# A selective state-space stack on one core: who adds up the scaled states, and in which order the projections run

## The chip, the cores and the metric

The program runs on one NeuronCore of a Trainium2 chip. Its five engines have queues of their own and meet at semaphores: TensorE (PE) for matrix products, VectorE (DVE), ScalarE (ACT), GpSimd (POOL) and SyncE (SP), which issues most DMAs. The metric is the device time of one execution in microseconds (us); a kernel is run several times and the median is compared.

## The reference

The input is one sequence x of 8192 positions with 512 channels, in fp32. Two parts follow, each as x + layernorm(part(layernorm(x))).

The first part is a stack of two Mamba layers, and it takes nearly all the time. With 1024 inner channels and 16 states each, a layer computes:

```python
xz = einsum('bld,ed->ble', x, W_in);  xc, z = split(xz, 2)
u = silu(causal depthwise conv of 4 taps (xc) + b_c)
dt, Bm, Cm = split(einsum('bld,ed->ble', u, W_x), [32, 48])
delta = softplus(einsum('blr,dr->bld', dt, W_dt) + b_dt)
dA = exp(delta * A);  dBu = delta * Bm * u
h = dA_t * h + dBu_t;  y_t = sum over n of h[:, n] * C_t[n]    # for every position t
y = (y + u * D) * silu(z);  out = einsum('bld,od->blo', y, W_out)
```

The second part is a soft mixture of 16 experts with 16 slots each. The change doesn't touch it.

## The kernel before, in words

A layer is cut into 16 chunks of T = 512 positions, so there are 32 chunks; the index G counts them. A chunk has 32 groups k: two halves of four 128-channel blocks, times 16 states. Each group needs four scans of 512 positions, one a block; VectorE does two blocks in one instruction (`scan`, L1289). So a chunk has 128 slots s = 4k + b, one for each scan of a block, and 64 double scans, p = s // 2. All orders are tables over these slots:

- ScalarE makes the decays exp(delta A) into a PSUM ring of four (`decay_of`, L928), and the first column of the scan's input (`head`, L938). It may be two double scans ahead.
- GpSimd makes the inputs delta u B (`inputs`, L1172) in a ring of three double scans.
- TensorE turns the states of a group, one 128-position tile j at a time, so that positions stand on the partitions (`turn_states`, L666). It writes the turned tile, 128 x 512, to one of two PSUM banks in turn (`BANK`, `turn_bank`); the bank is free when the engine that reads tile i - 2 is done.
- The turned tile is multiplied by C, one number per partition. VectorE does six of eight tiles and adds in the same instruction into `acc` (`add_state`, L1319; the first of a sum is a scaling, L1317). ScalarE does the others (`by_act`, `product`, L958) into one of three pairs of buffers `prod`. These are j = 0 of even k and j = 3 of odd k, `V_AT = (0, 3)`. A pair q is the two tiles of k = 2q and 2q + 1.
- GpSimd adds the pairs of a half to the first of them (`add_pair`, L1214: seven in a half), and at the half's end `join` (L1223) adds the total to `acc`. `V_SUM_AT` and `JOIN_AT` say behind which input each stands.
- TensorE turns the sum back (`turn_y`: a product with a diagonal of D, then four turned pieces added in PSUM), and VectorE multiplies it by silu(z) (`gate_y`, L1328). `Y_AT` has the slots of these y tiles.

Between these run the projections of this chunk and the next, in the order of `ORDER`. `timetable` gives each matmul a slot of TensorE by weights, and each result a slot in ScalarE's program, `TAKE_LAG` = 3 later plus what `TAKE_LATER` says. Two PSUM banks serve them in turn (`RING` = 2): a projection may start when ScalarE has taken the one two places ahead in `ORDER`. The silus need another table than the exponentials, so one is a table load, an activation over four blocks and a table load back (`silu_u`, `silu_z`); `SILU_LATER` moves the four of a chunk. By the table before, silu of z stands in ScalarE's slots 114 and 2 of the next chunk, silu of u in 42 and 66. `W_AT` has GpSimd's steps on delta (`sum_delta` L1154, `product` L1161), at p13, p16, p20, p23 and p46, p49, p52, p56.

The chunks G = 0 to 13 also carry the layernorm of chunk G + 2: its steps on ScalarE (`NORM_AT`) and four turned tiles on TensorE (`norm`, L694). Chunk 31 has no next chunk to project for.

## Time and profile before

| | us |
|---|---|
| median of 3 runs (7706.72 to 7708.32) | 7707.89 |
| the profiled execution | 7704.26 |
| its span | 7702.5 |
| VectorE busy in the span | 7066.7 (92%) |
| TensorE busy | 7011.1 (91%) |
| GpSimd busy | 6663.3 (87%) |
| ScalarE busy | 6029.3 (78%) |

The mean granted clock of TensorE is 0.982 of full speed. A row of the timeline gives the start (us from the span's start), the duration, engine, line of the kernel, operation, output and inputs, the number of instructions merged in it, and in brackets the idle time of the engine ahead of it with the instruction that the trace names as its end. A row that merges n instructions runs from the start of the first to the end of the last. Neighbouring instructions of an engine overlap a little, since the next is started before the last has written its end. The first scan starts at 100.4 us and the last at 7120.4 us.

### The profile page before, as it was taken

What the parts mean: (1) busy time and instruction counts of PE and PEld (TensorE: products, weight loads), DVE (VectorE), ACT (ScalarE), POOL (GpSimd) and SP (SyncE); (2) the same over time, 40 slices, a digit from 0 to 9 for tenths busy, and PEclk for the clock granted to TensorE, in tenths of its full rate; (3) what the DMA queues carried; (4) which work ended last, traced back from release to release, by engine and by line L of the source; (5) the groups of instructions that cost most, each with busy time, mean ns of one, the idle gap of its engine ahead of it and who ended that gap; (6) DMA issues with size and microseconds to landing.
All of it is one profiled execution on the core that took longest, in us unless ns stands there. A gap on an engine that the chain in (4) does not pass through costs nothing. (4 is left out here: it accounts for less than half of the span.)

```text
span 7702.5 us, 98947 instructions
## 1 busy us (share of the span) xinstructions
PE 7011.1 (91%) x29580; PEld 3860.8 (50%) x29580; DVE 7066.7 (92%) x6228; ACT 6029.3 (78%) x13267; POOL 6663.3 (87%) x3115
## 2 busy tenths in 40 slices
PE   7899999999999999999999999999999999987799
PEld 3444544544554454544554555444554544444664
DVE  5999999999999999999999999999999999999755
ACT  7788888888788888877888888777888887776564
POOL 5999999999999999999999999999999999998010
PEclk9999999999999999999999999999999999998999
DMA  3222222222222222222222222222222222221765
GB/s 107 77 85 84 79 85 72 79 85 81 86 78 86 78 73 83 83 87 70 87 88 69 76 69 77 73 75 70 75 77 68 76 71 73 76 72 52 257 229 183
DMA packets 282695, 684.05 MB, mean 89 GB/s; under 512 B 37872, under 2 KB 38128, under 8 KB 254384
## 3 DMA queue, kind: packets, MB, share of 16 engines
q1 hardware_dynamic: 252464, 626.31, 24.7%
q10 hardware_dynamic: 29696, 51.40, 1.8%
q8 instruction: 239, 3.92, 0.2%
q14 instruction: 296, 2.42, 0.1%
HBM read 508.76 MB, written 168.82 MB: 88 GB/s over the span
## 5 line engine op out<-in xcount | busy, mean ns | idle before, releaser
L1172 POOL TENSOR_TENSOR bu<-w,b_rep 128x1022 f32<-128x1022 f32 x2048 | 4797.9, 2361 | 416.6 <-DVE h L1289 413.1
L1289 DVE TENSOR_TENSOR_SCAN h<-decay,bu 128x1024 f32<-128x1024 f32 x2048 | 4644.0, 2277 | 216.0 <-ACT decay L928 71.0
L666 PEld LDWEIGHTS turn<-ident_m,h 128*128 128x128 f32 x16384 | 1963.2, 143 | 2697.1 <-issue 1287.4
L928 ACT ACTIVATE decay<-delta,neg_a 128x511 f32<-128x511 f32 x4096 | 2664.9, 684 | 738.8 <-DVE h L1289 735.6
L666 PE MATMUL turn<-ident_m,h 128*128 128x128 f32 x16384 | 2550.5, 280 | 489.5 <-DVE acc L1319 352.2
L1319 DVE SCALAR_TENSOR_TENSOR acc<-turn,c_now,acc 128x512 f32<-128x512 f32 x2816 | 1966.5, 733 | 139.8 <-PE turn L666 138.8
L1214 POOL TENSOR_TENSOR prod<-prod 128x1024 f32<-128x1024 f32 x448 | 1060.5, 2367 | 10.1 <-ACT prod L958 10.1
L588 PE MATMUL proj<-conv_in,conv_diag 128*128 128x512 f32 x1984 | 995.4, 601 | 67.6 <-ACT halo L818 67.6
L588 PE MATMUL proj<-x_conv,w_in 128*128 128x512 f32 x2048 | 1034.4, 602 | 9.3 <-ACT u L825 8.1
L588 PE MATMUL proj<-x_gate,w_in 128*128 128x512 f32 x2048 | 1012.4, 594 | 0.0
L958 ACT ACTIVATE prod<-turn,c_now 128x512 f32<-128x512 f32 x1024 | 696.3, 683 | 317.4 <-PE turn L666 296.5
L588 PE MATMUL proj<-zy,w_out 128*128 128x512 f32 x1024 | 518.5, 601 | 0.0
L588 PE MATMUL proj<-w_out,zy 128*128 128x512 f32 x1024 | 512.1, 599 | 0.9 <-DVE zy L1328 0.9
L938 ACT COPY bu<-h_first 128x2 f32<-128x2 f32 x2048 | 384.6, 188 | 63.8 <-ACT stage L877 26.2
L588 PEld LDWEIGHTS proj<-conv_in,conv_diag 128*128 128x128 f32 x1984 | 317.1, 191 | 213.5 <-ACT halo L818 107.8
L588 PEld LDWEIGHTS proj<-x_conv,w_in 128*128 128x128 f32 x2048 | 331.1, 193 | 141.8 <-issue 107.7
L588 PEld LDWEIGHTS proj<-x_gate,w_in 128*128 128x128 f32 x2048 | 327.3, 191 | 107.6 <-issue 107.6
L1154 POOL TENSOR_TENSOR delta<-delta,w 128x1024 f32<-128x1024 f32 x128 | 302.5, 2363 | 41.5 <-ACT w L862 41.5
L808 ACT ACTIVATE conv_diag<-ident_m,par 128x128 f32<-128x128 f32 x992 | 315.1, 390 | 0.4
L1161 POOL TENSOR_TENSOR w<-delta,u 128x1024 f32<-128x1024 f32 x128 | 303.4, 2370 | 0.3
L674 PE MATMUL turn<-u_back,d_diag 128*128 128x512 f32 x512 | 283.3, 635 | 2.5 <-DMA u_back<-u_rows 1.2
L588 PE MATMUL proj<-u,w_x 128*64 128x512 f32 x512 | 270.9, 623 | 10.2 <-ACT u L829 10.2
(167 smaller groups left out, 5721.6 us busy)
## 6 DMA issues: line engine op xcount, KB each, us to landing
b_rep<-b_rows SPq DMA_DIRECT2D x1024, 256.0 KB, 3.2
u_rows<-u SPq DMA_DIRECT2D x64, 1024.0 KB, 4.3
u_back<-u_rows SPq DMA_DIRECT2D x256, 256.0 KB, 3.5
x_gate<-xt SPq DMA_DIRECT2D x32, 1024.0 KB, 7.7
xt<-stage ACTq DMA_DIRECT2D x128, 256.0 KB, 2.4
x_conv<-xt SPq DMA_DIRECT2D x31, 1024.0 KB, 6.3
x_gate<-in_x_dram SPq DMA_DIRECT2D x16, 1024.0 KB, 5.1
x_l<-in_x_dram SPq DMA_DIRECT2D x16, 1024.0 KB, 10.0
```

The source lines that it names most:

```text
L588: mm = pe.matmul(out[0:lhs.shape[1], :], lhs, rhs, start=n == 0, stop=n == count - 1)
L666: mm = pe.transpose(out[:, b * P:(b + 1) * P], h[:, (G * GROUPS + k) % H_RING, b, j * P:(j + 1) * P], ident[:])
L808: act.activation(conv_diag[:, b % 2, k, :], ident[:], ACT.Copy, scale=par[:, STATES + k, b:b + 1])
L928: act.activation(decay[:, (G * SLOTS_BODY + s) % DEC_RING, 1:T], delta[:, blk, 1:T], ACT.Exp, scale=neg_a[:, n, blk:blk + 1]).then_inc(dec ...
L938: act.copy(bu[:, (G * PAIRS + p) % BU_RING, :, 0], h_first[:, hf, n, 2 * pr:2 * pr + 2]).then_inc(head_set, 1)
L958: act.activation(prod[:, V_BUFFER[q], k % 2, :], turn[:, BANK[tile], :], ACT.Copy, scale=c_now[:, j, n:n + 1]).then_inc(v_done, 1)
L1154: pool.tensor_tensor(delta[:, lo:lo + 2, :], delta[:, lo:lo + 2, :], w[:, lo:lo + 2, :], ALU.add).then_inc(delta_set, 1)
L1161: pool.tensor_tensor(w[:, lo:lo + 2, :], delta[:, lo:lo + 2, :], u[:, lo:lo + 2, :], ALU.mult).then_inc(w_set, 2)
L1172: pool.tensor_tensor(bu[:, (G * PAIRS + s // 2) % BU_RING, :, 1:T], w[:, blk:blk + 2, 1:T], b_rep[:, g % B_RING, 1:T].unsqueeze(1).to_broa ...
L1214: pool.tensor_tensor(total, total, prod[:, V_BUFFER[q]], ALU.add).then_inc(vsum_set, 1)
L1289: dve.tensor_tensor_scan(h[:, (G * GROUPS + k) % H_RING, 2 * pr:2 * pr + 2, :].rearrange("p b t -> p (b t)"), decay[:, at:at + 2, :].rearr ...
L1319: dve.scalar_tensor_tensor(out, src, scalar, out, ALU.mult, ALU.add).then_inc(x_done, 1)
```

## The change

- ScalarE's two tiles of a pair are now j = 3 of even k and j = 0 of odd k: `V_AT = (3, 0)`. Only for the first two groups of a half it is different: of k = 0 ScalarE takes both j = 3 and j = 0, and writes them into `acc` itself, and of k = 1 VectorE takes all four.
- Pair 1 of a half is written to that half's own total, and GpSimd adds pairs 2 to 7 to it, out of one spare buffer. There are no joins.
- `turn_y` adds six turned pieces: four of `acc`, two of the total. It waits for both.
- VectorE's first addition for j = 0 and j = 3 waits for ScalarE's tile in `acc`, and ScalarE's first write of a half waits for the last y tile of that half before.
- `ORDER` has the norm turns in other places, y weighs more, and takes, silus, y tiles, diagonals and two lists of loads and stores are moved. By the new tables silu of z stands in ScalarE's slots 110 and 126, silu of u in 46 and 62, and the y tiles of the second half in slots 16, 24, 32, 40.

```diff
@@ -41,19 +41,19 @@
-         ('conv_half', 7, 0), ('conv', 6, 0), ('conv', 7, 0), ('norm', 0, 0), ('out', 0, 0), ('norm', 1, 8),
-         ('out', 1, 0), ('x_proj', 0, 0), ('norm', 2, 0), ('norm', 3, 0), ('turn_c', 0, 0), ('delta_next', 0, 0),
-         ('delta_next', 1, 0), ('out', 2, 0), ('delta_next', 2, 0), ('delta_next', 3, 4), ('out', 3, 0), ('gate', 0,
+         ('conv_half', 7, 0), ('conv', 6, 0), ('conv', 7, 0), ('norm', 0, 0), ('out', 0, 0), ('out', 1, 0),
+         ('x_proj', 0, 0), ('norm', 1, 0), ('turn_c', 0, 0), ('delta_next', 0, 0), ('norm', 2, 0),
+         ('delta_next', 1, 0), ('norm', 3, 0), ('out', 2, 0), ('delta_next', 2, 0), ('delta_next', 3, 4), ('out', 3, 0), ('gate', 0,
 SLOTS_BODY = GROUPS * HB
 PAIRS = SLOTS_BODY // 2
 TAKE_LAG, TAPS_LEAD, XDBL_LAG, CONV_LAG, PROD_LAG = 3, 2, 3, 3, 2
-TAKE_LATER = {('out', 0): -1, ('gate', 0): 1, ('gate', 2): 2, ('turn_c', 0): -1, ('conv', 5): -1, ('delta', 5): -1}
-SILU_LATER = (6, 6, 4, 4)
-V_SUM_AT = (10, 10, 10, 10, 10, 10, 10, 9, 9, 9, 10, 10, 10, 10, 10, 9)
-JOIN_AT = (41, 72)
+TAKE_LATER = {('conv_half', 1): -1, ('conv_half', 2): -1, ('out', 0): 0, ('norm', 0): -1, ('gate', 0): 1, ('gate', 2): 2, ('turn_c', 0): -1, ('conv', 5): -1,
+              ('delta', 5): -1}
+SILU_LATER = (8, 2, 1, 0)
+V_SUM_AT = 9
 W_AT = {13: ('sum', 2), 16: ('product', 2), 20: ('sum', 3), 23: ('product', 3), 46: ('sum_next', 0), 49:
         ('product_next', 0), 52: ('sum_next', 1), 56: ('product_next', 1)}
@@ -76,12 +76,12 @@
-Y_AT = ((116, 118, 122, 124), (20, 28, 36, 44))
-DIAG_AT = {106: (0, 0), 110: (0, 1), 119: (0, 2), 121: (0, 3), 12: (1, 0), 17: (1, 1), 26: (1, 2), 34: (1, 3)}
-U_LOAD_AT = {25: [(0, 0)], 26: [(0, 1)], 30: [(0, 2)], 31: [(0, 3)], 3: [(1, 0)], 4: [(1, 1)], 7: [(1, 2)], 9: [(1, 3)]}
-U_STORE_AT = {12: 0, 18: 1}
+Y_AT = ((116, 118, 121, 124), (16, 24, 32, 40))
+DIAG_AT = {104: (0, 0), 108: (0, 1), 119: (0, 2), 122: (0, 3), 9: (1, 0), 13: (1, 1), 22: (1, 2), 30: (1, 3)}
+U_LOAD_AT = {25: [(0, 0)], 26: [(0, 1)], 30: [(0, 2)], 31: [(0, 3)], 2: [(1, 0)], 3: [(1, 1)], 6: [(1, 2)], 8: [(1, 3)]}
+U_STORE_AT = {13: 0, 18: 1}
@@ -110,7 +110,7 @@
-WEIGHT = {"x_proj": 1.1, "delta": 1.25, "delta_next": 1.25, "turn_c": 0.5, "norm": 0.5, "state": 0.55, "y": 1.6}
+WEIGHT = {"x_proj": 1.1, "delta": 1.25, "delta_next": 1.25, "turn_c": 0.5, "norm": 0.5, "state": 0.55, "y": 1.9}
@@ -164,20 +164,26 @@
 PROJ_PROLOGUE = NB + 1 + 1 + HB + NORM_AHEAD * KD
-V_AT = (0, 3)
+V_AT = (3, 0)
 HALF_Q = STATES // 2
-V_BUFFER = (0, 1, 2, 1, 2, 1, 2, 1, 2, 1, 0, 1, 0, 1, 0, 1)
+
+
+SPARE = 2
+V_BUFFER = tuple(q // HALF_Q if q % HALF_Q == 1 else SPARE for q in range(GROUPS // 2))
 def by_act(tile):
-    return tile[0] == "state" and tile[2] == V_AT[tile[1] % 2]
+    what, k, j = tile
+    if what == "state" and k % STATES < 2:
+        return k % STATES == 0 and j in V_AT
+    return what == "state" and j == V_AT[k % 2]
 def emptied_before(q):
-    old = max(o for o in range(-len(V_BUFFER), q) if V_BUFFER[o] == V_BUFFER[q])
-    pair = old % len(V_BUFFER)
-    return ("join", pair // HALF_Q) if pair % HALF_Q == 0 else ("pair", pair), old < 0
+
+    old = q - 1 if (q - 1) % HALF_Q > 1 else q - 3
+    return "pair", old % (GROUPS // 2)
 V_TAKE = [[] for _ in range(SLOTS_BODY)]
@@ -212,13 +218,11 @@
     at, carried = [[] for _ in range(PAIRS)], []
     for q in range(GROUPS // 2):
-        mine = [(4 * q + V_SUM_AT[q], ("pair", q))] if q % HALF_Q else []
-        if q % HALF_Q == HALF_Q - 1:
-            mine.append((JOIN_AT[q // HALF_Q], ("join", q // HALF_Q)))
-        for p, op in mine:
-            at[p % PAIRS].append(op)
+        if q % HALF_Q > 1:
+            p = 4 * q + V_SUM_AT
+            at[p % PAIRS].append(("pair", q))
             if p >= PAIRS:
-                carried.append(op)
+                carried.append(("pair", q))
     return at, carried
@@ in turn_y @@
-        def turn_y(out, joined, X, hf, b):
+        def turn_y(out, added, summed, X, hf, b):
             n = y_number(X, hf, b)
             pe.wait_ge(dd_set, n + 1)
             pe.wait_ge(uback_in[n % 2], (n // 2 + 1) * 16)
             pe.matmul(out, d_diag[:, n % 2, :], u_back[:, n % 2, :], start=True, stop=False)
-            pe.wait_ge(vsum_set, joined)
+            pe.wait_ge(x_done, summed)
             for j in range(J):
-                mm = pe.matmul(out[:, j * P:(j + 1) * P], acc[:, hf, j, b * P:(b + 1) * P], ident[:], start=False, stop=j == J - 1,
+                pe.matmul(out[:, j * P:(j + 1) * P], acc[:, hf, j, b * P:(b + 1) * P], ident[:], start=False, stop=False,
+                          is_transpose=True)
+            pe.wait_ge(vsum_set, added)
+            for odd in range(2):
+                j = V_AT[odd]
+                mm = pe.matmul(out[:, j * P:(j + 1) * P], prod[:, hf, odd, b * P:(b + 1) * P], ident[:], start=False, stop=odd == 1,
                                is_transpose=True)
             mm.then_inc(turn_full, 1)
@@ in turn_tile @@
-                turn_y(out, sum_base(G, kind) + (kind.sums.index(("join", x)) + 1 + C_PROD), G - x, x, j)
+                added = sum_base(G, kind) + (kind.sums.index(("pair", LAST_Q[x])) + 1 + C_PROD)
+                summed = dve_base(G, kind) + (kind.turns.by_dve["state", x * STATES + STATES - 1, J - 1] + 1 + C_TURN)
+                turn_y(out, added, summed, G - x, x, j)
@@ in product @@
-            emptied, in_last = emptied_before(q)
-            if k % 2 == 0 and not (kind.first and in_last):
-                behind = in_last and emptied not in SUMS_CARRIED
-                at = SUMS.index(emptied) - len(SUMS) if behind else kind.sums.index(emptied)
-                act.wait_ge(vsum_set, sum_base(G, kind) + (at + 1 + C_PROD))
-            act.activation(prod[:, V_BUFFER[q], k % 2, :], turn[:, BANK[tile], :], ACT.Copy,
-                           scale=c_now[:, j, n:n + 1]).then_inc(v_done, 1)
+            hf, begins = q // HALF_Q, q % HALF_Q == 0
+            if begins and j == V_AT[1] and not kind.first:
+                old = "y", hf, HB - 1
+                behind = TURN_TILES if hf == 0 else 0
+                act.wait_ge(turn_full, turn_base(G, kind) + (ALL_TURNS.index[old] + 1 - behind))
+            if k % 2 == 0 and q % HALF_Q > 1 and not (kind.first and q == 2):
+                act.wait_ge(vsum_set, sum_base(G, kind) + (kind.sums.index(emptied_before(q)) + 1 + C_PROD))
+            out = acc[:, hf, j, :] if begins else prod[:, V_BUFFER[q], k % 2, :]
+            act.activation(out, turn[:, BANK[tile], :], ACT.Copy, scale=c_now[:, j, n:n + 1]).then_inc(v_done, 1)
...
@@ in add_pair, join @@
-            total = prod[:, V_BUFFER[q - q % HALF_Q]]
-            pool.tensor_tensor(total, total, prod[:, V_BUFFER[q]], ALU.add).then_inc(vsum_set, 1)
-        def join(G, kind, op):
-            hf, done = op[1], sum_base(G, kind) + kind.sums.index(op) + C_PROD
-            pool.wait_ge(vsum_set, done)
-            last = "state", hf * STATES + STATES - 1, 2
-            pool.wait_ge(x_done, dve_base(G, kind) + (kind.turns.by_dve[last] + 1 + C_TURN))
-            both = acc[:, hf, V_AT[0]:V_AT[1] + 1:V_AT[1] - V_AT[0], :]
-            pool.tensor_tensor(both, both, prod[:, V_BUFFER[hf * HALF_Q]], ALU.add).then_inc(vsum_set, 1)
+            total = prod[:, q // HALF_Q]
+            pool.tensor_tensor(total, total, prod[:, SPARE], ALU.add).then_inc(vsum_set, 1)
@@ in add_state @@
@@ -1300,8 +1299,11 @@
             scalar, src, out = c_now[:, j, n:n + 1], turn[:, BANK[tile], :], acc[:, hf, j, :]
             if k == 0 or k == HALF_C:
                 dve.wait_ge(c_set, 2 * G + (k // HALF_C + 1))
+            begun = "state", hf * STATES, j
             first, before = False, ("state", k - 1 - by_act(("state", k - 1, j)), j)
-            if before[1] < hf * STATES:
+            if before[1] < hf * STATES and by_act(begun):
+                dve.wait_ge(v_done, act_base(G, kind) + (kind.turns.by_act[begun] + 1 + C_PROD))
+            elif before[1] < hf * STATES:
                 first = True
                 old = "y", hf, HB - 1
```

What moves, at three places. First GpSimd, in the second half of a second-layer chunk, from the input of p42 before (p38 after) to the first exponent of the next chunk; `delta<-delta,w` and `w<-delta,u` are the delta steps, `prod<-prod` a pair's sum. Before:

```order
L1172 TENSOR_TENSOR bu<-w,b_rep 128x2x511 x4
L1214 TENSOR_TENSOR prod<-prod 128x1024
L1154 TENSOR_TENSOR delta<-delta,w 128x1024
L1172 TENSOR_TENSOR bu<-w,b_rep 128x2x511 x3
L1161 TENSOR_TENSOR w<-delta,u 128x1024
L1172 TENSOR_TENSOR bu<-w,b_rep 128x2x511 x2
L1214 TENSOR_TENSOR prod<-prod 128x1024
L1172 TENSOR_TENSOR bu<-w,b_rep 128x2x511
L1154 TENSOR_TENSOR delta<-delta,w 128x1024
L1172 TENSOR_TENSOR bu<-w,b_rep 128x2x511 x2
L1181 TENSOR_TENSOR a_first<-neg_a,delta 128x64
```

and after:

```order
L1185 TENSOR_TENSOR bu<-w,b_rep 128x2x511 x8
L1167 TENSOR_TENSOR delta<-delta,w 128x1024
L1185 TENSOR_TENSOR bu<-w,b_rep 128x2x511 x3
L1174 TENSOR_TENSOR w<-delta,u 128x1024
L1185 TENSOR_TENSOR bu<-w,b_rep 128x2x511
L1227 TENSOR_TENSOR prod<-prod 128x1024
L1185 TENSOR_TENSOR bu<-w,b_rep 128x2x511 x2
L1167 TENSOR_TENSOR delta<-delta,w 128x1024
L1185 TENSOR_TENSOR bu<-w,b_rep 128x2x511 x2
L1227 TENSOR_TENSOR prod<-prod 128x1024
L1194 TENSOR_TENSOR a_first<-neg_a,delta 128x64
```

The sum of pair 9 ahead of the first delta step is gone (as is the join four inputs ahead of it), and the sums of pairs 10 and 11 stand one input earlier.

Then ScalarE in the same chunk, around the silu of u's second half, `u<-u`; `stage<-proj` is the take of output projection 0, `u<-proj,par` that of conv 7. Before:

```order
L958 ACTIVATE prod<-turn,c_now 128x512 x2
L938 COPY bu<-h_first 128x2
L928 ACTIVATE decay<-delta,neg_a 128x511 x2
L969 COPY h_last<-h 128x4
L877 COPY stage<-proj 128x512
L879 DMA xt<-stage 128x512
L938 COPY bu<-h_first 128x2
L928 ACTIVATE decay<-delta,neg_a 128x511 x2
L829 ACT_TABLE_LOAD
L829 ACTIVATE u<-u 128x2048
L772 ACT_TABLE_LOAD
L938 COPY bu<-h_first 128x2
```

and after:

```order
L837 ACTIVATE u<-proj,par 128x512
L950 COPY bu<-h_first 128x2
L940 ACTIVATE decay<-delta,neg_a 128x511 x2
L841 ACT_TABLE_LOAD
L841 ACTIVATE u<-u 128x2048
L784 ACT_TABLE_LOAD
L950 COPY bu<-h_first 128x2
L940 ACTIVATE decay<-delta,neg_a 128x511 x2
L982 COPY h_last<-h 128x4
L950 COPY bu<-h_first 128x2
```

The silu stood behind the take of output projection 0, and now stands behind conv 7, ahead of that take.

Last ScalarE at the start of a second-layer chunk: the silu of z's second half, `zy<-zy`, conv taps, `conv_diag`, and the first pair of scaled tiles. Before:

```order
L928 ACTIVATE decay<-delta,neg_a 128x511 x2
L871 ACT_TABLE_LOAD
L871 ACTIVATE zy<-zy 128x2048
L772 ACT_TABLE_LOAD
L808 ACTIVATE conv_diag<-ident_m,par 128x128 x4
L938 COPY bu<-h_first 128x2
L928 ACTIVATE decay<-delta,neg_a 128x511 x2
...
L958 ACTIVATE prod<-turn,c_now 128x512
L808 ACTIVATE conv_diag<-ident_m,par 128x128 x4
L958 ACTIVATE prod<-turn,c_now 128x512
```

and after:

```order
L940 ACTIVATE decay<-delta,neg_a 128x511 x2
L879 COPY zy<-proj 128x512
L883 ACT_TABLE_LOAD
L883 ACTIVATE zy<-zy 128x2048
L784 ACT_TABLE_LOAD
L950 COPY bu<-h_first 128x2
L940 ACTIVATE decay<-delta,neg_a 128x511 x2
...
L972 ACTIVATE prod<-turn,c_now 128x512 x2
L820 ACTIVATE conv_diag<-ident_m,par 128x128 x4
```

The silu has moved ahead by two double scans and stands behind gate 7. The two scaled tiles of a pair, which had taps between them, stand together.

## Rows read from the trace of the kernel before

**Rows 1.** Windows: busy time of each engine, one chunk each, last chunk third.

```profile
2326.32:2548.54 222.22, 203.45 (x870) 110.05 (x869) 209.42 (x169) 184.04 (x411) 206.95 (x98) 1.00 0.25 81
4519.92:4737.11 217.19, 201.51 (x853) 108.15 (x852) 208.99 (x169) 174.28 (x384) 206.56 (x97) 1.00 0.23 73
6910.62:7122.60 211.98, 163.00 (x694) 101.66 (x692) 207.40 (x167) 137.80 (x292) 192.97 (x87) 0.81 0.19 60
```

**Rows 2.** Timeline of GpSimd: the same join in two neighbouring chunks, twice.

```profile
2348.20 2.35 POOL L1223 TENSOR_TENSOR acc<-acc,prod 128x1024 f32<-128x1024 f32 x1
...
2570.42 2.36 POOL L1223 TENSOR_TENSOR acc<-acc,prod 128x1024 f32<-128x1024 f32 x1
...
4541.80 2.34 POOL L1223 TENSOR_TENSOR acc<-acc,prod 128x1024 f32<-128x1024 f32 x1
...
4758.99 2.35 POOL L1223 TENSOR_TENSOR acc<-acc,prod 128x1024 f32<-128x1024 f32 x1
```

**Rows 3.** VectorE's groups by line: shapes, count, busy us, mean ns, idle before.

```profile
L1289 DVE TENSOR_TENSOR_SCAN h<-decay,bu 128x1024 f32<-128x1024 f32 x2048 | 4644.0, 2277 | 216.0 <-ACT decay L928 71.0 <-PE turn L666 68.5 <-POOL bu L1172 64.1
L1319 DVE SCALAR_TENSOR_TENSOR acc<-turn,c_now,acc 128x512 f32<-128x512 f32 x2816 | 1966.5, 733 | 139.8 <-PE turn L666 138.8
L1317 DVE TENSOR_SCALAR acc<-turn,c_now 128x512 f32<-128x512 f32 x256 | 183.1, 736 | 19.7 <-PE turn L666 17.8
...
L1346 DVE TENSOR_SCALAR u<-conv_in,par 128x512 f32<-128x512 f32 x8 | 4.4, 547 | 28.9 <-ACT conv_in L816 28.9
```

**Rows 4.** GpSimd's groups by line: the sums of pairs.

```profile
L1214 POOL TENSOR_TENSOR prod<-prod 128x1024 f32<-128x1024 f32 x448 | 1060.5, 2367 | 10.1 <-ACT prod L958 10.1
```

**Rows 5.** Timeline of VectorE, second-layer chunk: scans p51, p52, p55 and p56.

```profile
4690.13 2.29 DVE L1289 TENSOR_TENSOR_SCAN h<-decay,bu 128x1024 f32<-128x1024 f32 x1 [0.45 <-POOL bu L1172]
...
4694.75 2.29 DVE L1289 TENSOR_TENSOR_SCAN h<-decay,bu 128x1024 f32<-128x1024 f32 x1 [1.03 <-PE turn L666]
...
4704.30 2.29 DVE L1289 TENSOR_TENSOR_SCAN h<-decay,bu 128x1024 f32<-128x1024 f32 x1 [0.27 <-POOL bu L1172]
...
4708.92 2.29 DVE L1289 TENSOR_TENSOR_SCAN h<-decay,bu 128x1024 f32<-128x1024 f32 x1 [1.02 <-ACT decay L928]
```

**Rows 6.** Timeline of GpSimd at the same place: inputs p51, p52 and p53, delta sum.

```profile
4687.58 2.35 POOL L1172 TENSOR_TENSOR bu<-w,b_rep 128x1022 f32<-128x1022 f32 x1
4689.89 2.35 POOL L1154 TENSOR_TENSOR delta<-delta,w 128x1024 f32<-128x1024 f32 x1
4692.20 4.66 POOL L1172 TENSOR_TENSOR bu<-w,b_rep 128x1022 f32<-128x1022 f32 x2
```

**Rows 7.** Timeline of ScalarE around silu of u, and VectorE's scans p34, p35.

```profile
4628.30 0.58 ACT L877 COPY stage<-proj 128x512 f32<-128x512 f32 x1 [2.23 <-PE proj L588]
...
4630.69 1.28 ACT L829 ACT_TABLE_LOAD   x1
4631.98 1.92 ACT L829 ACTIVATE u<-u 128x2048 f32<-128x2048 f32 x1
...
4635.31 1.29 ACT L928 ACTIVATE decay<-delta,neg_a 128x511 f32<-128x511 f32 x2
...
4636.69 4.47 DVE L1289 TENSOR_TENSOR_SCAN h<-decay,bu 128x1024 f32<-128x1024 f32 x2 [2.28 <-PE turn L666]
```

**Rows 8.** Timeline of VectorE in the chunk's start, and of ScalarE there.

```profile
4546.40 0.75 DVE L1319 SCALAR_TENSOR_TENSOR acc<-turn,c_now,acc 128x512 f32<-128x512 f32 x1 [0.75 <-PE turn L666]
...
4560.88 0.75 DVE L1319 SCALAR_TENSOR_TENSOR acc<-turn,c_now,acc 128x512 f32<-128x512 f32 x1 [0.98 <-PE turn L666]
...
4554.95 1.27 ACT L808 ACTIVATE conv_diag<-ident_m,par 128x128 f32<-128x128 f32 x4
4556.37 0.69 ACT L958 ACTIVATE prod<-turn,c_now 128x512 f32<-128x512 f32 x1
```

**Rows 9.** Timeline of TensorE and VectorE, first-layer chunk, around p38 and p39.

```profile
2464.01 0.66 PE L694 MATMUL proj<-ident_m,x_gate 128*128 128x128 f32 x4 [2.10 <-ACT spare_m L843]
...
2465.14 1.41 DVE L1319 SCALAR_TENSOR_TENSOR acc<-turn,c_now,acc 128x512 f32<-128x512 f32 x2 [2.08 <-PE turn L666]
```

18 lines of the change are left out of this document (7 added, 11 removed).

## The prediction

> **What bounds the kernel now.** I read the windows first, one for a chunk of each layer and one for the last chunk. In a first-layer chunk VectorE is busy 209.42 of 222.22 us, in a second-layer chunk 208.99 of 217.19 us; GpSimd follows with 206.95 and 206.56 us [rows 1]. The same GpSimd sum comes back after 222.22 us in the first layer (2348.20 to 2570.42) and after 217.19 us in the second (4541.80 to 4758.99), so these are the periods of a chunk [rows 2]. VectorE is the bound, and what can be won is its idle time: 12.80 us a chunk in the first layer, 8.20 us in the second. The state-space stage has 32 chunks. The 14 first of them carry the next chunks' normalization and have the long period; 17 have the short one; the last has no projections for a next chunk and takes 211.98 us [rows 1]. All idle time together is 14 x 12.80 + 17 x 8.20 = 319 us.
>
> Then I read VectorE's timeline for where it waits in a second-layer chunk, and the other engines at the same moments. I count a chunk's 64 double scans from p0 to p63.
> - Before p51, p52, p55 and p56 it waits 0.45, 1.03, 0.27 and 1.02 us, together 2.77 [rows 5]. The trace names GpSimd for two of them, TensorE and ScalarE for the others. But GpSimd has no gap there: the input of p51 is ready at 4689.93 and the scan starts at 4690.13; a delta sum of 2.35 us stands in front of the next input, which ends at 4694.5, and p52 starts at 4694.75 [rows 5, 6]. All four are GpSimd's.
> - Before p34 it waits 2.28 us [rows 7]. ScalarE waited 2.23 us for TensorE's output projection, then ran the silu of u with its two table loads (1.28 + 1.92 + 1.28 = 4.48 us) and came to the decays of p34 late. The trace names TensorE; but the decays end at 4636.60 (4635.31 + 1.29), and the scan starts at 4636.69.
> - The rest, 8.20 - 2.77 - 2.28 = 3.15 us, lies mostly in the first 24 scans, where an accumulation waits for a turned tile. The two longest are 0.75 and 0.98 us [rows 8]. There ScalarE is late: between the two scaled tiles of a pair it makes conv taps (1.27 us), and the tile it has not taken holds one of the two PSUM banks of the turns.
> - In the first layer there is 2.08 us more before the accumulations of p39: TensorE stands 2.10 us until ScalarE has emptied the x_proj bank, since two norm turns follow x_proj in one slot [rows 9]. 12.80 - 2.77 - 2.28 - 2.08 = 5.67 us are left for the rest there.
>
> **The change part by part.**
>
> GpSimd loses four of its 16 sums a chunk: the two joins and pairs 1 and 9. One takes 2.35 us [rows 2, 4], so GpSimd goes from 206.6 to about 197.3 us of work. The joins themselves are worth little: that of the second half sits at p8, that of the first at p41, ahead of places where GpSimd catches up again. What counts is pair 9 at p45, right ahead of the stretch in which four delta steps, at 2.35 us each, make GpSimd late. Worked from p43, where it is level with the scans: without pair 9 it has 2.35 us more, and the four waits of 2.77 us shrink to 0.4. But the silu of z's first half now stands at slot 110 instead of 114, behind three gates and a product that waits for GpSimd's sum. I expect ScalarE to be about 0.8 us late at p56. Gain 2.77 - 0.4 - 0.8 = 1.6 us. Ends: 0, if ScalarE takes over the whole wait, and 2.77.
>
> The silu of u's second half moves from slot 66 to 62, ahead of the take of out 0. ScalarE no longer waits 2.23 us ahead of it, and the scan behind it has two accumulations in front. The silu costs ScalarE 4.48 us and the next decays 1.3. When ScalarE is level, the decays of a scan are ready 3.4 us ahead of it, and the next scan starts 3.5 us later (a scan of 2.2 and two accumulations of 0.65): 6.9 against 5.8 us, so it just fits. I take 2.1 of the 2.28 us, with ends 0.5 and 2.3.
>
> The chunk's start: the silu of z's second half moves from slot 2 of the next chunk to slot 126, where ScalarE has lead, and two conv_half takes come a slot earlier. Each pair of scaled tiles now stands in neighbouring slots with nothing long between them (before, taps, a conv_half or an exponential stood there in most pairs). Adding up ScalarE's work from slot 126 on, with its durations from the timeline, I find it ahead of every scan of p0 to p12 by 1 us or more in the second layer, and level with it around p8 in the first, where the normalization's sums are added. Gain 2.4 of 3.15 us in the second layer, 4.2 of 5.67 in the first. Ends: 0 and all of it.
>
> The norm turns are spread over slots 77, 79 and 81. TensorE no longer has two of them behind x_proj, but the delta and norm takes of ScalarE now follow closely and each bank waits for one of them. Gain 1.0 of the 2.08 us, first layer only. Ends: -1.5 (three such round trips of about 1.2 us in a row) and 2.08.
>
> What it adds. Each of the eight y tiles gets six turned pieces instead of four. Four turns take 0.66 us [rows 9], so at most 0.33 us a tile, 2.6 us a chunk of TensorE, which is idle part of the time; I take 0.4 us on the path. Twelve waits are new: with one spare buffer, ScalarE may scale the next pair only when GpSimd has added the last. The sum stands in the same scan's place as the product that needs it. Behind the product in ScalarE's queue are the decays of the next scan, and in TensorE's the next turned tile, for which VectorE waits. GpSimd, when level, finishes such a sum about when ScalarE comes to the product. I take 0.3 us; ends 0 and 17 (below). VectorE's four first writes a chunk that were scalings (L1317) become multiply-adds (L1319): 736 against 733 ns [rows 3], nothing.
>
> Here the trace has to be weighed against a rule. In this kernel the same scaling of 512 columns takes 547 ns out of SBUF and 736 out of PSUM [rows 3], so the cheap form is not the one that is given up. The Trainium skill, "VectorE: DVE Perf Modes", section "The perf-mode tier table", gives fp32 tensor_scalar twice the speed of tensor_tensor; its section "Why PSUM operands drop a tier" takes that away for a PSUM operand. By the first alone the change would lose 128 x (733 - 547) ns = 24 us; by the second, as by the rows, nothing.
>
> The earlier loads of u_back on SyncE's queue move by one scan step; nothing waited for them, and their consumers move by the same four slots. ScalarE's count of products stays at 32 a chunk.
>
> **The sum.** First layer: 1.6 + 2.1 + 4.2 + 1.0 - 0.4 - 0.3 = 8.2 us a chunk. Second: 1.6 + 2.1 + 2.4 - 0.4 - 0.3 = 5.4. Together 14 x 8.2 + 17 x 5.4 + 1 for the last chunk = 207.6 us. The profiled execution took 7704.3 us; that gives 7496.7. The median of the runs is 3.6 us above the profiled one, so 7500 us. The last chunk supports the size: with no silu of u and no delta steps it already runs in 211.98 us, and the forecast for a second-layer chunk is 217.19 - 5.4 = 211.8.
>
> **The rivals.**
> - Only GpSimd's relief pays. ScalarE's lateness moves instead of going, since it does the same work in the same total. For it: ScalarE's silus still cost 4.48 us each and their lead is short. Against it: ScalarE is busy only 174.28 of 217.19 us [rows 1]. Then 31 x 1.6 = 50 us up to 31 x 2.77 = 86 go: 7622 to 7658 us, 7640.
> - Nearly all idle time goes: 290 of the 319 us, 7418 us. For it: the waits found all have a named owner which the change treats. Against it: each move brings a neighbour nearer.
> - Slower: the single spare buffer ties VectorE to GpSimd. Place: the 12 scans with a sum behind their input. If GpSimd's input for such a scan is only just ready, the sum ends 2.35 us after the scan starts; then come the product (0.69) and the turn (0.66), against a scan of 2.2 us (two in a row take 4.47 [rows 7]): 1.5 us of wait. For it: at p51 to p56 GpSimd is just in time in the kernel before [rows 5, 6]. Against it: with four sums fewer it is ahead by more than 1.5 us nearly everywhere. All twelve cost 17 us a chunk; the turn to slower comes when more than about five of them are late in every chunk. At seven or eight: 11 - 6.7 us x 31 = +140, some 7840 us.
> - No change: TensorE's order is the true limit and its waits close up behind every gap that is opened. 7708 us. Against it: its clock stands at 1.00 in these windows and its waits in the rows all end with ScalarE or VectorE.
>
> **How the numbers follow.** Forecast 0.62, only the relief 0.18, nearly all 0.08, slower 0.08, no change 0.04. The forecast's own range is 7440 to 7570 us; the range to hold 8 in 10 takes in most of the second case's neighbourhood and the edge of the third: 7415 to 7625. A measurement can tell 0.2% (15 us) from nothing. Faster by more 0.88, within 0.04, slower 0.08.
>
> **What would show it.** Right: GpSimd near 197 us a chunk with VectorE's waits before p51, p52 and p55 gone; no wait over 0.5 us behind the silu of u; chunk periods near 212 and 214 us; VectorE's busy time unchanged. Wrong: "ACT prod" waiting for GpSimd's sum in microseconds per chunk, with acc waiting for turns at the same scans; a wait of over 2 us behind a silu at its new slot; waits of TensorE for ScalarE around slots 79 to 82.

## Result, and the profile after

| | before | after |
|---|---|---|
| median of 5 runs each, us | 7707.98 (7706.72 to 7710.85) | 7745.21 (7733.93 to 7755.68) |
| the profiled execution | 7704.26 | 7733.93 |

The ratio is 1.0046, 95% interval 1.0031 to 1.0061: slower by 0.5%, where 2.7% faster was forecast. The time lies 120 us above the range. These five runs spread over 22 us, those of the kernel before over 4.

Windows of the kernel after; each runs from the start of a chunk's p0 to that of the next. The columns are those of [rows 1]. The first row is chunk 2, the second chunk 10, the third chunk 20, the fourth the last:

```profile
543.69:772.63 228.94, 210.13 (x887) 116.92 (x886) 210.47 (x169) 183.84 (x411) 197.98 (x94) 0.97 0.24 79
2353.56:2578.46 224.90, 205.63 (x887) 114.49 (x886) 210.41 (x170) 183.83 (x411) 198.09 (x94) 0.99 0.25 80
4556.96:4772.84 215.88, 201.76 (x871) 111.51 (x870) 209.30 (x169) 173.74 (x384) 197.86 (x93) 1.00 0.23 74
6939.71:7155.42 215.71, 166.45 (x710) 104.08 (x708) 207.53 (x168) 135.87 (x290) 182.26 (x82) 0.81 0.18 57
```

GpSimd has 198 us of work a chunk, as forecast (197). VectorE's is 1.0 us more in the first layer (210.41 against 209.42) and 0.3 in the second. But a first-layer chunk takes 224.90 us instead of 222.22 [rows 1], and three of them (2, 7 and 12) take 229. A second-layer chunk takes 215.9 or 217.5 in turn instead of 217.19, and the last one 215.71 instead of 211.98. VectorE still has its idle time; it has moved. The groups by line show where to:

```profile
L1288 DVE TENSOR_TENSOR_SCAN h<-decay,bu 128x1024 f32<-128x1024 f32 x2048 | 4641.3, 2278 | 77.3 <-POOL bu L1185 44.7 <-ACT decay L940 23.0 <-issue 7.3
...
L1321 DVE SCALAR_TENSOR_TENSOR acc<-turn,c_now,acc 128x512 f32<-128x512 f32 x2944 | 2085.5, 736 | 243.4 <-PE turn L671 239.0
...
L972 ACT ACTIVATE prod<-turn,c_now 128x512 f32<-128x512 f32 x896 | 606.0, 684 | 444.7 <-PE turn L671 347.3 <-POOL prod L1227 87.1 <-ACT stage L889 6.9
...
L1330 DVE TENSOR_TENSOR zy<-turn,zy 128x512 f32<-128x512 f32 x256 | 173.3, 677 | 76.6 <-PE turn L687 74.2
```

The scans wait 77.3 us instead of 216.0, and 44.7 of it is one wait ahead of the first chunk: GpSimd no longer holds them, and ScalarE's decays hold them for 23.0 us. The accumulations wait 243.4 instead of 139.8 [rows 3], and the gates of y, which had waited 14.2 us in all, wait 76.6. Nearly all of that ends with TensorE. Four places make 170 of these 320 us; a fifth kind of place comes behind them.

**p60, in every chunk.** VectorE's timeline in chunk 20, then TensorE's:

```profile
4756.60 2.28 DVE L1288 TENSOR_TENSOR_SCAN h<-decay,bu 128x1024 f32<-128x1024 f32 x1
4760.90 0.69 DVE L1330 TENSOR_TENSOR zy<-turn,zy 128x512 f32<-128x512 f32 x1 [2.02 <-PE turn L687]
```

```profile
4757.02 1.88 PE L593 MATMUL proj<-x_gate,w_in 128*128 128x512 f32 x4
4758.74 0.60 PE L671 MATMUL turn<-ident_m,h 128*128 128x128 f32 x4
4759.18 1.02 PE L679 MATMUL turn<-u_back,d_diag 128*128 128x512 f32 x2
4760.04 0.60 PE L682 MATMUL turn<-ident_m,acc 128*128 128x128 f32 x4
4760.48 0.38 PE L687 MATMUL turn<-ident_m,prod 128*128 128x128 f32 x2
```

The third y tile stands at slot 121 instead of 122. The two state tiles ahead of it are ScalarE's, so VectorE has nothing between its scan and the gate of y, while TensorE still has two products of a gate projection, a state tile and the y tile in front. The rows show another thing that I had not used: a product of 512 columns in fp32 is two records 0.43 us apart, 0.86 us together.

**p41, in the first layer.** TensorE, then VectorE, chunk 10; then VectorE in chunk 2:

```profile
2494.06 1.12 PE L646 MATMUL proj<-xdbl,w_dt 65*128 65x512 f32 x2 [1.75 <-ACT delta L866]
2495.02 0.60 PE L671 MATMUL turn<-ident_m,h 128*128 128x128 f32 x4
2495.46 0.60 PE L706 MATMUL proj<-ident_m,x_gate 128*128 128x128 f32 x4
2497.38 1.12 PE L593 MATMUL proj<-zy,w_out 128*128 128x512 f32 x2 [1.32 <-ACT delta L866]
```

```profile
2498.98 0.75 DVE L1321 SCALAR_TENSOR_TENSOR acc<-turn,c_now,acc 128x512 f32<-128x512 f32 x1 [2.69 <-PE turn L671]
2500.27 0.75 DVE L1321 SCALAR_TENSOR_TENSOR acc<-turn,c_now,acc 128x512 f32<-128x512 f32 x1 [0.55 <-PE turn L671]
...
691.79 0.75 DVE L1321 SCALAR_TENSOR_TENSOR acc<-turn,c_now,acc 128x512 f32<-128x512 f32 x1 [5.39 <-PE turn L671]
694.35 0.75 DVE L1321 SCALAR_TENSOR_TENSOR acc<-turn,c_now,acc 128x512 f32<-128x512 f32 x1 [1.81 <-PE turn L671]
```

Norm turns and delta steps are short, and each needs the bank that ScalarE takes two places earlier: a round trip for each. In chunk 2 VectorE's waits are two to three times as long. The windows say why, chunk 2 and then chunk 10; the third figure from the end is the granted clock:

```profile
687.50:697.50 10.00, 9.10 (x26) 4.84 (x26) 3.90 (x4) 6.72 (x15) 1.58 (x2) 0.65 0.45 157
2497.40:2507.40 10.00, 10.00 (x41) 5.65 (x42) 7.88 (x8) 7.22 (x15) 5.54 (x3) 1.00 0.52 171
```

At the same place of chunk 10 it is 1.00 (2.4 GHz) and TensorE gets 41 matmuls done in 10 us; in chunk 2 it is mostly at the lower level (1.2 GHz), with 26. It fell right behind TensorE's waits of 0.74 and 1.75 us; in chunk 10 nearly the same two waits (0.75 and 1.75) left it up.

**p29, in the first layer.** TensorE waits 1.03 us for the bank of conv 7, and VectorE 1.55. Norm 0 stands between conv 7 and out 0 in both kernels, but before a state tile came between norm 0 and out 0; now norm 0 is one slot later, right in front of out 0, and ScalarE has its two scaled tiles ahead of conv 7:

```profile
2456.05 1.12 PE L593 MATMUL proj<-zy,w_out 128*128 128x512 f32 x2 [1.03 <-ACT u L837]
...
2457.65 0.75 DVE L1321 SCALAR_TENSOR_TENSOR acc<-turn,c_now,acc 128x512 f32<-128x512 f32 x1 [1.55 <-PE turn L671]
```

**The chunk's edge, p1.** Behind the gate projections TensorE has little to do until the next chunk. In chunk 10 it idles 2.19 us, the clock falls, and VectorE waits 0.85 + 0.55 us:

```profile
2353.04 0.85 PE L671 MATMUL turn<-ident_m,h 128*128 128x128 f32 x4 [2.19 <-DVE acc L1321]
2353.68 1.92 PE L593 MATMUL proj<-x_conv,w_in 128*128 128x512 f32 x2
...
2358.87 0.75 DVE L1321 SCALAR_TENSOR_TENSOR acc<-turn,c_now,acc 128x512 f32<-128x512 f32 x1 [0.85 <-PE turn L671]
```

A state tile's 0.60 us has become 0.85 and a product's 1.02 is 1.92. TensorE idles 2.18 or 2.19 us at each of the 30 edges, and the clock falls at 20 of them; before the change it idled 1.75 us, and the clock fell at 11. Below, a fall is a stretch of over 2 us in which the trace shows products at this double spacing. In chunks 1 to 30 there are 17 falls before the change and 25 after it.

**Behind ScalarE's pair.** ScalarE's two tiles of a pair now stand in the two slots of every fourth double scan. VectorE waits for the next turned tiles one double scan later, at p9, p25, p37, p45, p49, p53 and p57. Two of these in chunk 20:

```profile
4707.82 0.75 DVE L1321 SCALAR_TENSOR_TENSOR acc<-turn,c_now,acc 128x512 f32<-128x512 f32 x1 [0.40 <-PE turn L671]
4747.25 0.75 DVE L1321 SCALAR_TENSOR_TENSOR acc<-turn,c_now,acc 128x512 f32<-128x512 f32 x1 [0.47 <-PE turn L671]
```

From p37 on they add up to 1.9 us a second-layer chunk and 2.0 a first-layer chunk; at the same places of the kernel before it was 0.15.

### The profile page after: what moved, and what is told of

It is laid out like the page before. It is cut to its first block and busy times, and to the rows that moved or that the text cites. A ratio compares the mean times of both kernels' runs of the same rounds, so it can differ in the third digit from the quotient of the medians.

```text
span 7732.1 us, 99686 instructions
## 1 busy us (share of the span) xinstructions
PE 7055.0 (91%) x30092; PEld 3974.9 (51%) x30092; DVE 7085.3 (92%) x6228; ACT 6018.2 (78%) x13267; POOL 6381.2 (83%) x2987
## 5 line engine op out<-in xcount | busy, mean ns | idle before, releaser
L1288 DVE TENSOR_TENSOR_SCAN h<-decay,bu 128x1024 f32<-128x1024 f32 x2048 | 4641.3, 2278 | 77.3 <-POOL bu L1185 44.7
L671 PEld LDWEIGHTS turn<-ident_m,h 128*128 128x128 f32 x16384 | 1993.0, 143 | 2588.5 <-issue 1464.4
L1321 DVE SCALAR_TENSOR_TENSOR acc<-turn,c_now,acc 128x512 f32<-128x512 f32 x2944 | 2085.5, 736 | 243.4 <-PE turn L671 239.0
L972 ACT ACTIVATE prod<-turn,c_now 128x512 f32<-128x512 f32 x896 | 606.0, 684 | 444.7 <-PE turn L671 347.3
L1227 POOL TENSOR_TENSOR prod<-prod 128x1024 f32<-128x1024 f32 x384 | 909.4, 2368 | 11.5 <-ACT prod L972 11.5
L646 PE MATMUL proj<-xdbl,w_dt 65*128 65x512 f32 x512 | 274.0, 618 | 35.6 <-ACT delta L866 24.9
```

The source lines that it names most:

```text
L671: mm = pe.transpose(out[:, b * P:(b + 1) * P], h[:, (G * GROUPS + k) % H_RING, b, j * P:(j + 1) * P], ident[:])
L972: act.activation(out, turn[:, BANK[tile], :], ACT.Copy, scale=c_now[:, j, n:n + 1]).then_inc(v_done, 1)
L1227: pool.tensor_tensor(total, total, prod[:, SPARE], ALU.add).then_inc(vsum_set, 1)
L1288: dve.tensor_tensor_scan(h[:, (G * GROUPS + k) % H_RING, 2 * pr:2 * pr + 2, :].rearrange("p b t -> p (b t)"), decay[:, at:at + 2, :].rearr ...
L1321: dve.scalar_tensor_tensor(out, src, scalar, out, ALU.mult, ALU.add).then_inc(x_done, 1)
```

## The experiments

Each was run beside the kernel before; all times are medians. The interval of each ratio to it is 0.001 to 0.002 to either side, so two variants run at different times are told apart from some 10 us on; below that I go by the chunks' times.

**e1: the third y back at slot 122.**

```diff
-Y_AT = ((116, 118, 121, 124), ...     119: (0, 2), 122: (0, 3)
+Y_AT = ((116, 118, 122, 124), ...     119: (0, 2), 121: (0, 3)
```

> The changed kernel with the third y tile of the first half one turn slot later, at 122 as before the change, and the diagonal of the fourth at 121. My theory: the changed kernel's wait of 2.02 us ahead of that y's gate (p60, every chunk) comes from the slot 121, right behind ScalarE's two scaled tiles, so it falls to 0.5 us or less: 1.5 to 2 us x 32 = 48 to 64 us less than the changed kernel, 7680 to 7700 us. Rival, TensorE's load: the y tile's six pieces are late wherever they stand, the wait moves to the neighbouring accumulations or the next y, and the time stays within 15 us of 7745.

7692.0 us (0.9982, 0.9972 to 0.9992): 53 less. The wait is 0.50 us now. The edit does a little more than it says: by the tables gate 7 also ends at slot 121 instead of 123, and its take and the silu of z come two slots earlier, at 124. And only the first layer gained: its chunks take 221.8 us instead of 224.9, those of the second 216.1 and 217.4, as before the mend. In the second layer the clock falls at most edges, and VectorE comes to p1 earlier and waits 2.15 + 0.55 us there; at most edges of the first it no longer falls. So the 53 us mix the y tile with the clock. TensorE's timeline at the edge of chunk 20, and its window:

```profile
4516.37 0.66 PE L671 MATMUL turn<-ident_m,h 128*128 128x128 f32 x4 [0.24 <-DVE acc L1321]
4519.39 1.11 PE L671 MATMUL turn<-ident_m,h 128*128 128x128 f32 x4 [2.36 <-DVE acc L1321]
4520.30 1.91 PE L593 MATMUL proj<-x_conv,w_in 128*128 128x512 f32 x2
4522.00 1.06 PE L671 MATMUL turn<-ident_m,h 128*128 128x128 f32 x4
4522.85 3.18 PE L593 MATMUL proj<-x_conv,w_in 128*128 128x512 f32 x4
```

```profile
4517.00:4526.00 9.00, 6.64 (x17) 3.64 (x17) 7.37 (x5) 5.73 (x15) 8.03 (x4) 0.62 0.21 66
```

**e2: the old order of norm turns.** `ORDER` as before, `('out', 0): -1` in `TAKE_LATER`.

> The changed kernel with the old order of norm, out, x_proj and delta steps (two norm turns behind x_proj, takes of out 0 and norm 0 as before). My theory: the spread norm turns cost three round trips TensorE to ScalarE behind p41 (2.69 + 0.55 us of VectorE's wait), and norm 0 ahead of out 0 the 1.55 us at p29. Both go and the old wait of about 2.1 us at p39 comes back: first-layer chunks 1.5 to 3 us shorter, x 14, and with them the three chunks of 229 us: 25 to 50 us less than the changed kernel, 7695 to 7720 us; the second layer unchanged. Rival, the loss in the first layer is spread over the chunk (TensorE's load): within 10 us of 7745.

7836.8 us (1.0171): 92 more than the changed kernel. The order moved gates and deltas by a slot or more in both layers (gate 7 from 119 to 115), and chunk 20 got waits of 2.6 us at p41 and at p53. It tells nothing of the norm turns; it shows what a few slots cost. e13 and e16 hold all other slots.

**e3 and e4: the data flow alone, the tables alone.** e3 has the changed code with `ORDER`, `TAKE_LATER`, `SILU_LATER`, `Y_AT`, `DIAG_AT`, the loads and `WEIGHT` of before; e4 is the reverse.

> The changed data flow alone (no joins, first tiles into the accumulators, one spare buffer, six pieces a y) with all tables of the kernel before (order, takes, silus, y slots, weights). My theory, the tables lost the time: the relief of GpSimd shows here, waits before p51, p52 and p55 are gone, 30 to 85 us less than the kernel before: 7620 to 7680 us. Rival, the single spare buffer or the longer y cost it: as slow as the changed kernel or slower, 7740 to 7850 us, with waits of ScalarE's products for GpSimd's sums.

> The kernel before with the tables of the changed one (order, takes, silus, y slots, weights) and its own data flow, joins and three buffers. My theory, the tables lost the time: it is slower than the changed kernel, which at least has the relief: 7770 to 7850 us, with the long waits behind p41 and at p60. Rival, the data flow lost it and the tables gain: 7600 to 7700 us.

8216.7 us (1.0665) and 8020.6 (1.0411): both theories of e3 fell, and e4 lies above both of its own ranges. I had left out that the data flow comes with `V_AT = (3, 0)`. It puts ScalarE's two tiles of a pair into neighbouring slots, where they stood seven slots apart, and the old tables have takes and silus there. Leaving the swap out was not run; by the tables it has a price too: with tiles 0 and 3 the first product of the next pair comes one slot behind the second of this one, and with one spare buffer GpSimd's sum (2.35 us) would have to fit between.

**e6: the swap and the new tables, with joins.**

```diff
-V_AT = (0, 3)
+V_AT = (3, 0)      # and all tables of the changed kernel, V_SUM_AT 9
```

> The kernel before (joins, three buffers in turn, four pieces a y) with the changed kernel's tables and its swap of ScalarE's two tiles (state tile 3 of even steps, 0 of odd ones, in neighbouring slots). Against the changed kernel it differs by the data flow alone. If the tables only fit the swapped tiles, the 275 us that the tables alone cost (8021 against 7745) are gone. My theory: the flow is worth the relief, so this one is 30 to 60 us slower than the changed kernel, 7775 to 7805 us, with GpSimd late at p51 to p56. Rival, the flow itself loses (one spare buffer, longer y): below 7740 us.

7765.4 us (1.0074). Against e4 the swap, with most sums one input earlier, takes 255 us off: the tables fit the swapped tiles only. Against the changed kernel the old data flow (joins, three buffers, four pieces) costs 20 us, under my 30 to 60. That is far less than the 74 of e5 for the same four sums; the longer y and the one spare buffer are in this difference too, and other tables around it.

**e5: the relief of GpSimd alone.**

```diff
+            if q % HALF_Q == 1:
+                pool.sem_inc(vsum_set, 1)
+                return
...
-            pool.tensor_tensor(both, both, prod[:, V_BUFFER[hf * HALF_Q]], ALU.add).then_inc(vsum_set, 1)
+            pool.sem_inc(vsum_set, 1)
```

> The kernel before, with all its tables, in which GpSimd leaves out the four sums of a chunk that the change takes away (pairs 1 and 9, both joins; their parts are missing in y); it only signals them. It prices the relief alone. The prediction's term: 1.6 us a chunk, ends 0 and 2.77: 50 us less than the kernel before (7657), at most 86 (7621), with GpSimd's waits at p51 to p56 gone. Rival, TensorE and ScalarE are so nearly full that they take over: within 20 us of 7707.

7634.1 us (0.9901): 74 less than before. Chunk 20 takes 214.91 us, and of the four waits of [rows 5] 0.60 is left, before p56:

```profile
4480.31:4695.22 214.91, 202.24 (x855) 109.78 (x854) 208.80 (x170) 174.15 (x384) 197.70 (x93) 0.99 0.23 74
```

**e7: y with four pieces.** `turn_y` leaves out the two matmuls of `prod`.

> The changed kernel without the two extra pieces of each y tile (ScalarE's totals are missing in y). It prices the prediction's term of 0.4 us a chunk. My theory: TensorE has 0.2 us less per y tile, most of it in places with slack: 5 to 20 us less than the changed kernel, 7725 to 7740 us, the wait at p60 still 1.8 us. Rival, TensorE's work bounds the chunk: all eight tiles show, 8 x 0.22 x 31 = 55 us less, 7690 us.

7706.3 us (7697 to 7753): 39 less, which neither theory said. In the second layer nothing changed (216.6 us a chunk on average in both); the chunks of 229 us are gone. So most of it need not be the pieces' own. That needed e14.

**e8: TensorE's idle edge filled.** e1, and:

```diff
+                if s == 0 and not kind.first and kind.has("conv_half"):
+                    spare_bank = bank(G, kind, 0)
+                    for n in range(16):
+                        pe.transpose(spare_bank[:, n % J * P:(n % J + 1) * P], ident[:], ident[:])
```

> The changed kernel with the third y at slot 122, and 16 turns of the identity into a free projection bank at slot 0 of each chunk, where TensorE stood idle for 2.36 us. In the kernel with y at 122, the granted clock stands at half for some microseconds behind that idle time in most chunks and VectorE waits 2.15 us at p1 instead of 0.85. My theory: the idle time made the clock fall; filled, the clock stays up, p1 waits 0.9 us or less, 1 to 1.3 us in some 16 to 20 chunks: 15 to 30 us less than the kernel with y at 122 (7692), 7660 to 7677. Rival, the fill delays the turn behind it and the clock falls anyway: 7692 or more.

7642.6 us (0.9914, 0.9899 to 0.9929): 49 less than e1, more than I had said. TensorE and its window at the edge of chunk 20:

```profile
4487.87 1.91 PE L737 MATMUL proj<-ident_m 128*128 128x128 f32 x16
4490.40 0.65 PE L671 MATMUL turn<-ident_m,h 128*128 128x128 f32 x4 [0.62 <-DVE acc L1325]
4490.89 1.02 PE L593 MATMUL proj<-x_conv,w_in 128*128 128x512 f32 x2
```

```profile
4488.00:4497.00 9.00, 8.38 (x48) 5.56 (x47) 9.00 (x8) 7.42 (x22) 8.04 (x4) 1.00 0.26 68
```

The clock stays up, and VectorE is busy for all 9 us. One fall is left in chunks 1 to 30, where e1 had 23, and from chunk 2 on every chunk of a layer takes the same time, 221.8 and 214.5 us (within 0.4). More work for TensorE made the kernel faster. The Trainium skill, "TensorE: Matmul & The Clock Gate", section "HAM oscillation — how this bites in real kernels", describes the like: waits for DMAs between groups of matmuls put the clock back in every turn of a loop. The trace agrees that a wait does it. But the wait here is shorter than those of the page, 2.36 us, and the fall doesn't come in every turn: in e1 it came at 19 of 30 edges with the same wait at each.

**e11 and e12: the fill in the kernel before and in the changed kernel.**

> The kernel before with the same 16 turns filled in at slot 0 of each chunk. Its granted clock stood at half for over 2 us in a row at the chunk's edge in 11 of 31 chunks and behind p39 in two. My theory: where the fall did not lie on VectorE's path it costs nothing: 0 to 15 us less than the kernel before, 7692 to 7708. Rival: the fill costs TensorE 1.7 us a chunk that it does not have: 20 to 50 us slower.

> The changed kernel, y still at 121, with the 16 turns filled in at slot 0. My theory: the halved clock behind the idle edge costs the changed kernel the three chunks of 229 us (3 x 4) and 1.4 to 1.6 us in some 19 chunks: 35 to 45 us less than the changed kernel, 7700 to 7710; first-layer chunks all near 223.5, second-layer near 216. Rival, the clock falls for another reason (the long waits behind p41): the 229 us chunks stay and less than 20 us go.

e11: 7704.7 us (1.0000). The falls at the edge are gone and the time is the same, so they lay off VectorE's path. Nine falls are left, four at p39 where there were two. e12: 7717.8 us (1.0017, 1.0008 to 1.0027), 27 less than the changed kernel, between my two cases. The second layer is even at 215.8, the chunks of 229 are gone, but at p41 the clock now falls in 12 of 13 chunks (225.6 us). So the falls there don't hang on the edge's.

**e9: two takes of ScalarE a slot earlier.** e8 with `('conv', 7): -1`, `('delta_next', 0): -1`.

> The kernel with y at 122 and the filled slot 0 (e8), in which ScalarE takes conv 7 and delta_next 0 one slot earlier (59 and 81). In first-layer chunks out 0 waits for the bank of conv 7 because norm 0 stands between them, and VectorE waits 1.55 us at p29; behind p41 VectorE waits 2.69 + 0.55 us while TensorE waits three times for ScalarE's takes. My theory, round trips of banks: the 1.55 us go and p41 falls by 0.5 to 1 us, 1.5 to 2.5 us in each of 14 chunks: 20 to 35 us less than e8 (7643), 7608 to 7623, the second layer unchanged. Rival, ScalarE's queue is the limit there and its products come later instead: within 8 us of e8.

7641.5 us: nothing in the sum, the rival's number but not its reason. Where the clock stayed up (chunk 4) it did what I said: p29 fell from 1.55 to 0.43, p41 from 2.69 to 2.37, the chunk from 221.8 to 220.4. But it now falls at p41 in 9 of 13 chunks, which then take 221.8 or 223.4.

**e10: the second half's y tiles at 18, 26, 34, 42.** e8 with these in `Y_AT`, silu of u kept at 46.

> The kernel with y at 122 and the filled slot 0 (e8), with the second half's y tiles at slots 18, 26, 34, 42 instead of 16, 24, 32, 40: two slots behind the first of ScalarE's two tiles instead of between the two. My theory, as at p60: the place beside ScalarE's pair costs the waits of 0.28 + 0.55 us at p9 and p17 and 0.55 at p9 in the second layer; they fall to 0.3 or less: 0.3 to 1 us a chunk, 10 to 30 us less than e8 (7643). Rival, the projections pushed aside (conv 1 to 4 by a slot) bring new waits of the same size: within 8 us of e8 or slower.

7633.6 us: 9 less. VectorE's accumulations no longer wait at p9 and p17, nor the scan of p24 (0.85); before the scan of p9 there is now 0.22 us in the second layer and 0.79 in the first, for ScalarE's decays. A second-layer chunk takes 213.8 instead of 214.5. A first-layer chunk takes 0.5 more: the clock falls at p41 in 12 chunks, where it was one.

**e13, e16: the norm turns away from the delta steps.** All other tiles keep their slots. e13 is on e10, e16 on the changed kernel.

```diff
-norm 0 to 3 at slots 58, 77, 79, 81;  ('out', 0): 0, ('norm', 0): -1
+norm 0 to 3 at slots 58, 64, 70, 77;  ('out', 0): -2, ('out', 1): -2, ('norm', 0): -1, ('conv', 7): -1
```

> The kernel with y at 122, the filled slot 0 and the second half's y at 18, 26, 34, 42 (e10), with the norm turns moved to slots 58, 64, 70 and 77 instead of 58, 77, 79 and 81, all other tiles in the slots they had; conv 7 is taken a slot earlier, out 0 and out 1 two slots earlier, at 64 and 70. My theory: the norm turns among the delta steps make the round trips at p41 (4.2 + 1.5 us in a first-layer chunk, nothing in a second-layer one) and norm 0 the 1.55 us at p29. Then first-layer chunks fall from 222.3 to 216 to 218 us, the second layer stays at 213.8, in all 60 to 85 us less than e10 (7634): 7550 to 7575. Rival, the earlier takes hold ScalarE up and stop TensorE at slots 64 and 70 instead: 7600 to 7640, with new waits at p32 and p35.

> The changed kernel as it is (y at 121, nothing filled in), with only the norm turns moved to slots 58, 64, 70, 77 and the takes that this wants (conv 7 one slot, out 0 and out 1 two slots earlier). It prices the prediction's term for the norm turns in the changed kernel itself. My theory: 4 to 6 us in each of 14 first-layer chunks less, and 12 for the three of 229 us; 1 us in each second-layer chunk more for the early takes: 50 to 75 us less than the changed kernel, 7670 to 7695. Rival, the idle chunk edge makes the clock fall in more chunks instead: 7710 to 7740.

e13: 7577.1 us (0.9836, 0.9824 to 0.9849), 57 less than e10. First-layer chunks fell from 222.3 to 216.8; nothing is left at p41. The earlier takes cost the second layer 1.1 us a chunk, at p33 and p35. e16: 7708.5 us (1.0000, 0.9991 to 1.0010), 37 less than the changed kernel, less than I had said: first-layer chunks fell from 224.9 to 221.7, but those of the second rose to 218.6, since the clock now falls at the edge of every one (30 falls in chunks 1 to 30).

**e14 and e15: the y pieces and GpSimd's sums, with the clock held.** e14 is e8 with the edit of e7; e15 is e8 in which GpSimd only signals its twelve sums.

> The kernel with y at 122 and the filled slot 0 (e8) without the two extra pieces of each y tile (ScalarE's totals are missing in y). Without them the changed kernel was 39 us faster, but its clock fell less often too. If the pieces themselves cost 39 us, this one is near 7604; my theory, most of that was the clock's: 5 to 20 us less than e8 (7643), 7623 to 7638. Rival, TensorE's work bounds the chunk: 55 us less, 7588.

> The kernel with y at 122 and the filled slot 0 (e8), in which GpSimd leaves out all twelve sums a chunk and only signals them (their parts are missing in y): ScalarE then never waits for a spare buffer and GpSimd has 28 us a chunk less. It prices all that is left of GpSimd and of the single spare buffer. My theory, the rival of the single spare is wrong: 0 to 20 us less than e8 (7643), 7623 to 7643, mostly at p53. Rival, the spare buffer costs up to 1.5 us at several of the twelve: 50 us or more less.

7656.7 and 7659.6 us: both *slower* than e8 by 14 and 17, with less work. Windows of chunks 10 and 20, e14, then e15:

```profile
2326.58:2548.04 221.46, 203.94 (x887) 113.45 (x886) 210.06 (x169) 183.85 (x411) 197.96 (x94) 1.00 0.26 81
4501.19:4715.70 214.51, 201.88 (x871) 111.40 (x870) 209.27 (x169) 173.85 (x384) 197.87 (x93) 1.00 0.23 74
```

```profile
2336.26:2561.54 225.28, 209.60 (x903) 117.97 (x902) 210.18 (x170) 183.99 (x411) 171.16 (x82) 0.98 0.26 80
4516.19:4729.32 213.13, 202.57 (x887) 113.33 (x886) 209.16 (x169) 173.99 (x384) 171.00 (x81) 1.00 0.24 75
```

The pieces cost 0.3 us in an undisturbed first-layer chunk (221.8 to 221.46) and nothing in the second. The sums and the one spare buffer together cost 1.4 us in a second-layer chunk (214.5 to 213.1). Both kernels lose it again at p41, where the clock falls in 4 and in 12 of the first-layer chunks; e14 has 10 more falls, at p9 and at the edge.

One sign that I had named as wrong did come in the changed kernel: ScalarE's products wait 87.1 us for GpSimd's sums, 2.7 a chunk. By e15 VectorE feels half of it: without the sums the waits before p24, at p53 and at p57 of a second-layer chunk fall from 1.7 to 0.5 us.

**e17 and e18: the takes by layer, with and without the fill.** e17 is e13 in which chunks without a normalization take out 0 and out 1 at 66 and 72; e18 leaves out the fill.

> The kernel with the norm turns moved, y at 122 and 18, 26, 34, 42 and the filled slot 0 (e13), in which chunks without a normalization take out 0 and out 1 at their old slots 66 and 72. In e13 their second-layer chunks rose from 213.8 to 214.9 us, with waits at p33 and p35. My theory, the early takes made these: second-layer chunks back at 213.8, 17 x 1.1 = 19 us less than e13 (7577), 7558, the first layer at 216.8. Rival, it was the earlier take of conv 7, which stays: 7577.

> The same as e17 without the 16 turns filled in at slot 0. My theory: the edge's idle time of over 2 us makes the clock fall as in the kernel with y at 122 alone, 1.3 us or more at p1 in most chunks, and further falls at other places: 20 to 45 us slower than e17, 7580 to 7605. Rival, with no long waits left inside the chunk the clock stays up without the fill: within 8 us of e17.

e17: 7557.8 us (0.9804, 0.9790 to 0.9819), faster than both kernels. e18: 7600.8 (0.9861): 43 more without the fill, with 30 falls in chunks 1 to 30 where e17 has none. Windows of e17, chunks 10, 20 and the last:

```profile
2264.93:2481.68 216.75, 206.23 (x903) 114.74 (x902) 210.31 (x169) 183.19 (x411) 198.04 (x94) 1.00 0.27 84
4413.98:4627.73 213.75, 203.70 (x887) 112.96 (x886) 209.83 (x170) 173.92 (x384) 197.78 (x93) 1.00 0.23 75
6765.31:6978.55 213.24, 165.73 (x710) 103.77 (x708) 207.83 (x168) 135.91 (x290) 181.91 (x82) 0.82 0.18 58
```

A second buffer pair, as the direct test of the spare buffer, was not tried. Nor were the fill, the norm turns and the takes of e17 in the kernel before, so how much of e17's gain is the new data flow's and how much the tables' is not known.

## Why the prediction was wrong

By its own steps, in us a chunk:

- **GpSimd's relief** (1.6): right, too small. 74 / 31 = 2.4 (e5); the waits before p51, p52 and p55 are gone.
- **Silu of u** (2.1): right. The 2.28 us of [rows 7] are gone, 0.23 is left at p36.
- **The chunk's start** (2.4 and 4.2): this step failed, and it is the largest error of the sum, about 105 of the 245 us between forecast and measurement. I summed ScalarE's work and found it in time for p0 to p12. In the second layer it was; there VectorE waits for TensorE. At p24 the scan waits 0.87 us for ScalarE's decays, which I had not looked at. In p0 to p26 the waits were 2.8 us in the second layer and 4.2 in the first; they are 1.9 or, with a fall, 3.3 in the second, and 4.7 in the first. So 0.9 at best instead of 2.4, and -0.6 instead of 4.2. The 5.67 us that I took for the first layer's start also held 1.5 us of other places: the wait before p34 is 2.89 us there, not 2.28. The new y slots stand between ScalarE's two tiles (0.7 a second-layer chunk, e8 to e10), and the clock falls at the edge.
- **The norm turns** (1.0): wrong sign, at the end that I had named (-1.5) and beyond. 2.08 us at p39 [rows 9] became 3.24 at p41 and, new, 1.55 at p29 (0.37 before at p32): -2.3 instead of 1.0. Moving them away, with the takes of conv 7, out 0 and out 1 that this wanted, is worth 3.2 to 5.5 in a first-layer chunk (e16, e13).
- **The y pieces** (-0.4): right, 0 to -0.3 (e14). **The spare buffer** (-0.3): too small, up to -1.4 in the second layer (e15, with the sums' own time in it; in the first the falls hide it). That is far from the 17 of its bound; the slow rival, single spare, was not what happened. (Its sum has a slip: 4.3 x 31 is 133, not 140.)
- **Not in the sum: the pair itself.** I counted only a gain for ScalarE's two tiles in neighbouring slots. VectorE's waits behind them from p37 on are 1.9 to 2.0 us a chunk where there was 0.15, some 55 us in all; without the sums (e15) 1.2 of the 1.9 stay. They take back most of what the relief gave. No run takes the swap out of the changed kernel.
- **Not in the sum at all:** the third y tile. I costed the edit of `Y_AT` with its loads, not with what stands around the new slot. It costs 2.02 instead of 0.50 us in every chunk. With the clock held a second-layer chunk takes 1.3 us more for it (215.8 in e12, 214.5 in e8), some 40 us in all.
- **Not in the argument at all:** the clock. I had "its clock stands at 1.00 in these windows" as evidence against a limit by TensorE. It is evidence only for the kernel before. Each longer wait that the change gave TensorE could halve its speed for 3 to 10 us behind it; the fill is worth 27 us in the changed kernel (e12).

The rival nearest to the truth was "TensorE's order is the true limit and its waits close up behind every gap", to which I gave 0.04. I argued against it that all waits in the rows end with ScalarE or VectorE, and read a busy TensorE (203 of 222 us [rows 1]) as one with room. Part of that room is real: the same data flow, with y, norm turns and takes placed otherwise and the clock held, takes 7557.8 us, 150 of the 208 us forecast. But that needed moves which the prediction doesn't have, so it is no support for the sum.

The account from the changed kernel to e17, in order: the fill -27 (e12), the third y -75 (e8; -53 without the fill; both with falls in them), the second half's y -9 (e10), the norm turns and takes -76 (e17): -187.

## What to carry to other kernels

A table that moves a tile by one slot has to be costed by its neighbours: who works while the mover's engine gets to it. Where TensorE is as busy as here (91%) and still waits, look at its spacing in the windows behind each wait, not at the mean clock (0.98 here); a fill where it idles, into a bank that is free anyway, costs little and can be tried first. And a partial undo is only a test if the rest fits it: e2, e3 and e4 measured tables that no longer matched their tiles.

## What was not expected of the hardware

- A single idle stretch of 2.2 to 2.4 us of TensorE, with shorter waits ahead of it, was followed by a granted clock at half for 3.4 to 6.8 us (changed kernel, e1); waits of 0.74 and 1.75 us by up to 10 us of it (p41). In the same kernel the same place falls in some chunks and not in others, with the same waits. The kernel with 25 falls has runs 22 us apart, e17, with none, 1 us; that the falls make the spread is likely and not shown.
- Taking work away from TensorE or GpSimd made the kernel slower by 14 and 17 us (e14, e15), by falls at another place. Why the falls move from one place to the other stays open.
